# Two-layer gated attention and expert kernel: the first norm moved to GpSimd, two copies dropped, TensorE's attention loop written out, the scatter a step later

## What is computed

```python
x = x + jnp.tanh(g_xattn[0]) * _L0_xattn_ref(_layernorm(x, axis=-1), ctx_2048, w_qkv, w_proj, b_proj)
x = x + jnp.tanh(g_ffn[0]) * _L0_ffn_ref(_layernorm(x, axis=-1), ...)
# in _L0_xattn_ref: k, v = context's and own rows; softmax(q k) v, then the projection
# in _L0_ffn_ref, with its second layernorm's rows as x:
logits = x @ gate_w
top_id = jnp.argmax(logits, axis=-1)
score = jax.nn.sigmoid(top_val)
xs = x * score
routed = (silu(xs @ rt_gate[top_id]) * (xs @ rt_up[top_id])) @ rt_down[top_id]
return shared(x) + routed
```

## Time and profile before

| | us |
|---|---|
| median of 3 runs | 497.3 |
| the three runs | 490.04, 497.3, 498.94 |
| the profiled execution: span | 490.0 |
| PE busy in the span | 443.7 (91%) |
| DVE busy | 366.8 (75%) |
| POOL busy | 319.4 (65%) |
| ACT busy | 277.8 (57%) |

### The profile page before, as it was taken

How to read it: one execution, slowest core, us unless ns; L and a number is a source line. 1 busy time by engine, 2 the same in 40 slices (tenths; PEclk the granted TensorE clock), 3 DMA queues, 4 the chain that set the end, 5 groups by cost and what they waited for, 6 DMA issues and landing times. The chain is left out here.

```text
span 490.0 us, 20510 instructions
## 1 busy us (share of the span) xinstructions
PE 443.7 (91%) x6871; PEld 349.2 (71%) x6872; DVE 366.8 (75%) x1201; ACT 277.8 (57%) x775; POOL 319.4 (65%) x780
## 2 busy tenths in 40 slices
PE   5789999989999999997987999987997799899998
PEld 3456677756766666774666988864655799898997
DVE  3668999978898989944768666545766678788984
ACT  2468899877988888764234545434233434444431
POOL 3845765567777777767723666577825899898630
PEclk9889999998999999989999999998999699999999
DMA  7941231111111110100245776631000011111001
GB/s 232 413 152 41 48 36 27 26 31 40 28 32 33 30 36 22 37 20 18 76 131 158 228 227 216 222 121 37 18 5 13 16 46 33 46 37 37 23 23 33
DMA packets 37394, 37.38 MB, mean 76 GB/s; under 512 B 20440, under 2 KB 31504, under 8 KB 36816
## 3 DMA queue, kind: packets, MB, share of 16 engines
q0 software_dynamic: 7552, 20.20, 12.9%
q1 hardware_dynamic: 29200, 16.06, 11.9%
q10 hardware_dynamic: 576, 0.26, 0.2%
HBM read 24.82 MB, written 7.86 MB: 67 GB/s over the span
## 5 line engine op out<-in xcount | busy, mean ns | idle before, releaser
L979 DVE TENSOR_REDUCE negm<-PS 128x4 f16<-128x512 f32 x128 | 81.9, 681 | 0.4
L716 ACT ACTIVATE pexp<-PS 128x512 f32<-128x512 f32 x128 | 69.4, 595 | 6.4 <-PE PS L1383 5.8
L1725 PE MATMUL PS<-w,vp 128*128 128x128 f32 x512 | 63.3, 277 | 0.0
L1725 PEld LDWEIGHTS PS<-w,vp 128*128 128x128 f32 x512 | 60.6, 194 | 0.0
L1396 PEld LDWEIGHTS PS<-pexp,vp 128*32 128x32 f32 x2048 | 34.5, 113 | 26.4 <-issue 20.5
L1396 PE MATMUL PS<-pexp,vp 128*32 128x64 f32 x2048 | 50.3, 230 | 0.3
L1619 PE MATMUL PS<-xsT,wst 128*128 128x128 f32 x320 | 44.4, 282 | 3.0 <-DVE stack L1217 1.3
L1619 PEld LDWEIGHTS PS<-xsT,wst 128*128 128x128 f32 x320 | 38.8, 191 | 7.3 <-issue 5.0
L581 POOL DMA_INDIRECT sorted_x<-VALL,posu x32 | 33.3, 1040 | 13.4 <-issue 7.6
L611 POOL DMA_DIRECT2D wst<-in_rt_gate_up_dram x40 | 21.5, 538 | 29.2 <-PE PS L1619 19.9
L1310 DVE TENSOR_TENSOR vp<-PS,xnT 128x1024 f32<-128x1024 f32 x32 | 38.6, 1205 | 0.8 <-PE PS L1702 0.8
(11 more groups left out here) (246 smaller groups left out, 1254.5 us busy)
## 6 DMA issues: line engine op xcount, KB each, us to landing
wst<-in_rt_gate_up_dram POOLq DMA_DIRECT2D x40, 256.0 KB, 3.5
xs<-sorted_x SPq DMA_DIRECT2D x40, 64.0 KB, 2.8
sorted_y<-YS POOLq DMA_DIRECT2D x40, 64.0 KB, 3.0
out_dram<-X SPq DMA_DIRECT2D x32, 64.0 KB
X<-in_x_dram SPq DMA_DIRECT2D x1, 1536.0 KB, 8.2
CK<-in_ctx_k_dram SPq DMA_DIRECT2D x1, 1536.0 KB, 12.2
CV<-in_ctx_v_swapped_dram SPq DMA_DIRECT2D x1, 1536.0 KB, 16.6
rdn<-in_rt_down_dram POOLq DMA_DIRECT2D x1, 1024.0 KB, 10.6
```

Of the source, the lines that this page charges most:

```text
L716: nc.scalar.activation(pexp[:, j, :], PS[:, 2 + j % 2, :], ACT.Exp).then_inc(S["exped"], 1)
L979: dve.tensor_reduce(negm[:, a.par, :, j], PS[:, j % 2, :].rearrange("p (g k) -> p g k", g=G), AX.X, ALU.max, negate=True).then_inc(S["maxe ...
L1725: nc.tensor.matmul(PS[:, 6 + y.par, 0:D], z[:, y.par, e, :], w1[:, e * D:e * D + D], start=(e == 0), stop=False)
```

## The change

- First norm: POOL writes xn right behind rstd in its own step, waiting for its own root and for PE's transpose of two tiles before. DVE no longer has it, and waits ahead of bn_aggr until the norm of two tiles before is done (normed).
- Second norm: DVE writes it straight into XN2, once POOL has spread that tile's v (v_spread). xr and POOL's copy of it are gone, and what waited for r_kept waits for r_normed. PE transposes from XN2.
- The router's matmul reads XNT; xrT and ACT's copy into it are gone, and so is ACT's wait for r_routed.
- The scatter has stage 17 instead of 16 and stands in POOL's step behind the bias, ahead of the scaling and the one-hot sums; the vp copies wait for a - 13 scatters. POOL's program has one step more.
- PE's attention steps are all written out (looped=False). DVE, ACT and SP keep their loops.

```diff
-                l, f, a, m, c, k, e, o = (stage(i) for i in (0, 1, 4, 7, 9, 13, 14, 16))
+                l, f, a, m, k, e, o = (stage(i) for i in (0, 1, 4, 7, 13, 14, 17))
...
-                            if a.t > 12:
-                                pool.wait_ge(scattered, 16 * (a.t - 12))
+                            if a.t > 13:
+                                pool.wait_ge(scattered, 16 * (a.t - 13))
...
                         .then_inc(S["rstd_ready"], 1)
+                    pool.wait_ge(S["rstd_ready"], l.done())
+                    pool.wait_ge(S["xnT_done"], l.freed())
+                    pool.tensor_scalar(xn[:, l.par, :], X[:, l.cols(D)], mv[:, l.par, 0:1],
+                                       rstd[:, l.par:l.par + 1], ALU.subtract, ALU.mult).then_inc(S["normed"], 1)
...
-                if c:
-                    pool.wait_ge(S["r_normed"], c.done())
-                    pool.tensor_copy(XN2[:, c.t, 0:D], xr[:, c.par, :]).then_inc(S["r_kept"], 1)
+                if o:
+                    pool.wait_ge(S["k_placed"], o.quad_done(2, 1))
+                    pool.wait_ge(S["k_score"], o.quad_done(2, 1))
+                    pool.indirect_dma_start(out=sorted_x,
...
-                    pool.wait_ge(S["r_kept"], k.done())
+                    pool.wait_ge(S["r_normed"], k.done())
...
-            walk_flat(NT, 16, step)
+            walk_flat(NT, 17, step)
...
-                    act.wait_ge(S["r_routed"], c.freed())
                     act.wait_ge(S["r_xnT_done"], c.done())
-                    nc.scalar.copy(xrT[:, c.par, :], PS[:, 6, 2 * P:3 * P])
                     nc.scalar.copy(XNT[:, c.cols(P)], PS[:, 6, 2 * P:3 * P]).then_inc(S["r_xnT_kept"], 1)
...
                 if l:
+                    dve.wait_ge(S["normed"], l.freed())
                     dve.wait_ge(S["stats"], l.done())
...
-                    dve.wait_ge(S["r_xnT_done"], c.freed())
-                    dve.wait_ge(S["r_kept"], c.freed())
+                    dve.wait_ge(S["v_spread"], c.done())
                     dve.wait_ge(S["r_copied"], c.done())
-                    dve.tensor_scalar(xr[:, c.par, :], X[:, c.cols(D)], mvr[:, ds(c.t, 1)],
-                                      rstdr[:, ds(c.t, 1)], ALU.subtract, ALU.mult).then_inc(S["r_normed"], 1)
+                    dve.tensor_scalar(XN2[:, ds(c.t, 1), 0:D], X[:, c.cols(D)],
+                                      mvr[:, ds(c.t, 1)], rstdr[:, ds(c.t, 1)], ALU.subtract, ALU.mult)\
+                        .then_inc(S["r_normed"], 1)
...
-                if l:
-                    dve.wait_ge(S["xnT_done"], l.freed())
-                    dve.wait_ge(S["rstd_ready"], l.done())
-                    dve.tensor_scalar(xn[:, l.par, :], X[:, l.cols(D)], mv[:, l.par, 0:1],
-                                      rstd[:, l.par:l.par + 1], ALU.subtract, ALU.mult).then_inc(S["normed"], 1)
...
-                    nc.tensor.matmul(PS[:, 6, at:at + E], xrT[:, rl.par, :], gatew[:, 0:E], start=True, stop=True)\
+                    nc.tensor.matmul(PS[:, 6, at:at + E], XNT[:, rl.cols(P)], gatew[:, 0:E], start=True, stop=True)\
...
-                    nc.tensor.transpose(PS[:, 6, 2 * P:3 * P], xr[:, rt.par, :], identf).then_inc(S["r_xnT_done"], 1)
+                    nc.tensor.transpose(PS[:, 6, 2 * P:3 * P], XN2[:, rt.t, 0:D], identf).then_inc(S["r_xnT_done"], 1)
...
-            walk(pe, NT, 13, step, drain=shared_in_drain)
+            walk(pe, NT, 13, step, drain=shared_in_drain, looped=False)
```

More of the change, by code:

```diff
@@ L350, in flamingo_gated_two_layers @@
         stack_turned = [sem("a_stack_turned0"), sem("a_stack_turned1")]
-        for n in "stats moments var_eps copied normed kept xnT_done xnT_kept routed".split():
+        for n in "stats moments var_eps copied normed xnT_done xnT_kept routed".split():
             S["r_" + n] = sem("r_" + n)
@@ L487, in _ @@
         def _(pool):
[L488 to L490 removed]
+            credit(pool, ("rstd_ready", 1), ("normed", 1), ("var_eps", 1), ("bias_added", 1), ("v_spread", 1),
+                   ("v_half", 1), ("r_copied", 1), ("r_var_eps", 1))
             quad_credit(pool, ("k_score", 2), ("k_summed", 3))
@@ L894, in _ @@
         def _(dve):
-            credit(dve, ("stats", 1), ("moments", 1), ("normed", 1), ("lo_ready", 1), ("ctx_stacked", 1),
+            credit(dve, ("stats", 1), ("moments", 1), ("lo_ready", 1), ("ctx_stacked", 1),
                    ("k_kept", 1), ("maxed", 4), ("recip_ready", 1),
```

15 lines of the change are left out of this document (3 added, 12 removed).

## The result

| | before | after |
|---|---|---|
| median of 4 runs | 493.67 us (489.88 to 498.94) | 507.75 us (506.3 to 523.72) |
| profiled execution, span | 490.0 us | 505.2 us |
| its time | not on record | 506.7 us |

The ratio is 1.029, 95% interval 1.023 to 1.035: slower by about 3%, where 488.4 us was forecast and 496.0 was the range's upper end. The forecast of a gain of 8.9 us on the profiled execution met a loss of 15.2, span against span. An execution that ran at a lower granted clock than the kernel's others, such as the one of 523.72 us, counts in the medians given here but not in the ratios, so the two can differ by some tenths of a per cent.

A forecast was written before the change was run, and what follows sets the result against it. Bound: TensorE's own pace plus a VectorE-GpSimd-VectorE-TensorE handshake in the attention stage. Gains of 7.7 (16 steps), 0.7 (three earlier steps) and 0.5 (fill) total 8.9 us, 497.3 to 488.4; range 478.5 to 496.

The forecast's parts named there:

- I take 0.45: Attention stage, GpSimd: assumed 0.45 us for the 128x128 norm, from a copy at 0.296 and a two-tensor add at 0.461.
- Slack 0.4: Attention step: xn done on GpSimd at about 145.6, TensorE wanting it at 145.98, so 0.4 us to spare.
- After the multiply GpSimd starts its next step some 0.7 late, which the earlier moments cover: Attention quad, GpSimd: 0.7 us of lateness after the 128x512 multiply was to be absorbed by VectorE delivering moments earlier.
- filler between the scatter's issue and the copy: GpSimd's step: multiply (1.06 us) and sums (0.8) after the scatter's issue give its landing time before the vp copy waits.
- in each of four choosing steps: Attention loop: 0.2 us left as remaining loss in each of four steps where VectorE chooses experts, taken off the gain.
- rival C: GpSimd waits for a 4.0 us scatter landing each step; TensorE stops 0.8 and loses clock: 508 us, chance 0.05.
- A: Rival: the handshake moves, TensorE waits for xn from GpSimd; costs 4 us, gain 4.9, 492.4 us, chance 0.15.
- 16 steps at 5.79: Attention loop: TensorE's own pace of 5.79 us gives 92.6, with ranks 93.5, against 102.4 today; 8.9 at most.
- ScalarE at 0: Attention stage: ScalarE losing one 128x128 copy per step and the wait for r_routed was costed at 0 us.
- The first scatter and the fill: First scatter's TensorE stop shrinks from 1.60 to 0.3 or 0.4 us, keeping the clock; the fill gains 0.5.
- Whose span fills the whole of it within 0.1: Base: the profiled execution's span of 490.0 us was matched to the shortest of three times, 490.04.
- the median of three, 497.3: Base of the forecast: median of 490.04, 497.3 and 498.94 us, from which the gain of 8.9 was subtracted.

The follow-up runs named there:

- Experiment 1: Changed kernel with the one-hot sums moved back ahead of the scatter, the norm still on GpSimd: 494.41 us, ratio 1.006 to the kernel before.
- Experiment 4: Changed kernel with only the first norm returned to VectorE, scatter early and sums behind it: 492.57 us, ratio 0.995 to the kernel before.
- experiment 3: Kernel before with one edit, the first norm moved from VectorE to GpSimd behind its root: 502.57 us, ratio 1.031.
- experiment 8: Changed kernel with 24 matmuls of zeros ahead of TensorE's three waits in each choosing step: 502.47 us, ratio 1.029 to the kernel before.
- experiment 5: Changed kernel with the first norm back on VectorE and the sums ahead of the early scatter: 490.44 us, ratio 1.000; repeated, 489.94 us, 0.997.
- experiment 2: Changed kernel with the scatter back at its old place and lag, the norm still on GpSimd: 509.77 us, ratio 1.039 to the kernel before.
- experiment 7: Kernel before with TensorE's attention steps written out and nothing else changed: 493.5 us, ratio 1.005.
- the padded kernel: Changed kernel with norm on VectorE, sums ahead of scatter, and 34 do-nothing instructions in ScalarE's code: 491.83, 486.65, 486.72 us; ratios 0.985, 0.987, 0.988.
- the 502.42: Kernel before, unchanged, measured beside the first two kernels with 34 do-nothing instructions: 502.42 us; later against itself, 490.4 and 491.45 us.

## Why the prediction was wrong, point by point

**The norm's price.** The step that failed first is the term "I take 0.45". It measured 0.80 (796 to 972 ns), inside the stated ends of 0.3 and 1.06 but 0.35 over the value taken. I had reasoned that a norm has one tensor input. The Trainium skill, GPSIMD Engine Reference, "4.1 Engine selection", gives about 2x VectorE's time for two inputs and near line rate for one: VectorE's 0.40 twice is what was measured, though the operation has one tensor input and two scalars per partition. By its second half the page would have given 0.4, which these rows contradict.

**The slack.** "Slack 0.4" for xn was all but gone with 0.35 of extra norm alone. The step "After the multiply GpSimd starts its next step some 0.7 late, which the earlier moments cover" failed outright: VectorE's moments are there at 155.76, GpSimd comes to them at 157.23, 1.5 us late, and has no wait left that could cover anything. From there to the end of the norm it takes 3.9 us where the prediction had 3.4, and xn is 0.90 late.

**The sums.** The largest error is one of order, and it is in the diff for all to see: the sums went behind norm and scatter. I counted their busy time (0.8 a quad) and used them as filler between the scatter's issue and the copy, and never asked who waits for them. VectorE's choice does, and behind it all of VectorE. The 0.2 us "in each of four choosing steps" stood for a stop of 2.81 on VectorE and 2.7 on TensorE. Experiment 1 shows it: 14.4 us of loop. Experiment 4 shows that it needs the norm's 0.80 as well: behind the scatter but without the norm the sums cost nothing. The norm does cost without them, some 4 us of loop with the early scatter and 10.5 with the late one (experiment 3).

**The clock.** The forecast kept it at 1.00 after the fill. It fell to 0.50 for some 10 us in each of three quads, 9.3 of the loop's 14.9 us net, 12.2 in those quads (experiment 8). I had charged a half clock only in rival C, and only 1 us of it in every second step.

**The rivals.** A ("the handshake moves rather than goes") was the mechanism: TensorE waits for xn from GpSimd. Its price of 4 us left out the sums and the clock. Experiment 1, which is A almost without these two, takes 494.41 us where the same kernel with the norm on VectorE takes 490.44 (experiment 5): there the price is 4.0, as stated. C's time, 508, is nearly the one measured, but its cause, a wait for the landing in each step, is absent in the changed kernel; it appears when the scatter goes back behind the multiply (experiment 2, 1.23 us). A right number from a wrong mechanism, so luck.

**The pace.** "16 steps at 5.79" was too low as well. The cleanest loop that I ran, 115.7 us for 19 steps in the second profile of experiment 5, is 6.09 a step, at a clock of 1.00; its longest step in each quad still takes 6.5 to 6.9. Of the 8.4 us that the forecast took from the loop, some 4 were to be had (120.5 to 116.6), by the early scatter and the dropped copies, and none by writing TensorE out (experiment 7).

**The drain and ScalarE at 0.** ScalarE's loss of a copy was costed at 0. Its slow issue holds TensorE for 2.87 us there (0.81 in the padded kernel), and the first transpose of sorted rows starts 11.5 instead of 9.6 us behind the last scatter. That is the 2.0 us lost behind the loop.

**The first scatter and the fill.** Half right: near 110 us no half clock is left, and the fill gained 1.6 instead of 0.5. But the stop was to shrink from 1.60 to 0.3 or 0.4; TensorE still stands 0.30 and 1.12 us in that quad's choosing step, again behind VectorE's wait for the sums (1.32 there).

**The base.** "Whose span fills the whole of it within 0.1" did not hold: in all executions whose time and span are both on record 1.5 us lie outside the span (506.7 against 505.2), so the profiled one was not the one of 490.04. And the median of three, 497.3, was high: apart from the 502.42, more runs of before gave medians of 490.4 to 494.6. Both touch the level of 488.4, not the gain of 8.9, which failed by itself.

## What to carry to other kernels

Before an operation is moved to an engine, list for every instruction behind it on that engine who waits for it, the small ones above all: three sums of 0.2 us, moved behind an issue that itself follows a late norm, cost 14 us here. Where a TensorE near its limit is made to stop, price the stop and the half clock after it apart; filling the stops with idle matmuls tells the two from each other in one run, if what the added matmuls cost in quads that had kept their clock is counted apart. And a part of a change that looks free may be worth keeping only in another order: the same edits without the norm, with the sums first, beat both kernels, though before only with ScalarE's code padded to its old length.

## What the runs showed of the chip that was not expected

Stops of 0.90, 0.69 and 1.11 us on TensorE within some 5 us are followed by a granted clock of 0.50 for some 10 us, during which it is busy without a gap. In experiment 1 stops of up to 0.9 mostly left the clock at 1.00.

Thirty-four instructions that do nothing, in ScalarE's code, make one DMA issue fall from 2.13 to 0.43 us and the kernel up to 0.9% faster (0.997 to 0.988 of before, from runs made at different times); 3.9 us of that are seen at TensorE's first transpose of sorted rows. Why the issue is slow stays open.

The fill varies from one execution to the next: the 13th transpose started between 74.3 and 80.5 us in profiles of the same kernel (experiment 5: 80.53, then 74.27), with a granted clock of 0.84 and 1.00 in the first 40 us. These 6.3 us are most of the 6.9 by which the two spans differ, so an effect of under 1% is not seen in a single profile's total; the loop's length shows it better.
